# Edge arrays in rows of 2 KB, and routing and experts in one block: a graph layer on one core

## The reference

```python
xn = layernorm(x)
h = xn @ weight_l
agg = segment_sum(edge_weight[:, None] * h[dst], src, 12500)      # scatter-add by source
x = x + (agg + bias_l + xn @ weight_r + bias_r) + mix(xn)         # mix: linear attention, gated
xn2 = layernorm(x) * gamma + beta
logits = xn2 @ Wr + br                                            # 8 experts
top_vals, top_idx = top_k(logits, 2); w = softmax(top_vals)
out = x + sum over the two chosen experts e of w_e * (gelu(xn2 @ W1[e] + b1[e]) @ W2[e] + b2[e])
```

## Time and profile before

| | us |
|---|---|
| median of three runs | 4451.65 (4448.86 to 4453.43) |
| the profiled execution, its own time | 4440.3 |
| its span in the trace | 4438.6 |
| first scatter-add to the end of the last | 157.54 to 3257.14 |
| first instruction of the expert part on TensorE | 3651.79 |
| GpSimd busy | 3111.7 (70%) |
| TensorE busy | 3389.3 (76%), mean granted clock 0.864 |

### The profile page before, as it was taken

One profiled execution on the slowest core, in us unless ns is written; L12 is line 12 of the kernel. 1 busy time (PEld: TensorE's weight loads), 2 busy tenths in 40 slices (PEclk: granted clock), 3 DMA queues, 4 the chain that ended last, 5 costly groups with the idle time before them and its releaser, 6 DMA issues. The chain is left out here.

```text
span 4438.6 us, 85552 instructions
## 1 busy us (share of the span) xinstructions
PE 3389.3 (76%) x16628; PEld 2802.7 (63%) x16629; DVE 2495.7 (56%) x11386; ACT 1685.6 (38%) x3095; POOL 3111.7 (70%) x2088
## 2 busy tenths in 40 slices
PE   1466666667677677878888888888758859999998
PEld 1355555555565555666666666666557758888887
DVE  3577777665555555666666666666548862222222
ACT  1233333344444443444444444444312224444443
POOL 0488888888888888888888888888855544444444
PEclk7788878788888888888888888888779979999999
DMA  9888888877777777777777777777789965565554
GB/s 380 241 146 155 152 148 147 157 117 118 116 109 115 116 113 114 102 108 108 105 104 107 108 103 105 108 107 102 91 217 296 294 187 143 139 145 141 141 140 114
DMA packets 588869, 638.95 MB, mean 144 GB/s; under 512 B 60524, under 2 KB 553156, under 8 KB 587138
## 3 DMA queue, kind: packets, MB, share of 16 engines
q0 software_dynamic: 279264, 269.84, 48.5%
q1 hardware_dynamic: 262234, 273.19, 20.9%
q10 hardware_dynamic: 47304, 95.18, 5.9%
HBM read 249.82 MB, written 390.09 MB: 144 GB/s over the span
## 5 line engine op out<-in xcount | busy, mean ns | idle before, releaser
L818 POOL DMA_INDIRECT agg<-msg,sidx x1664 | 2585.7, 1554 | 667.5 <-issue 408.7
L1122 PE MATMUL bank<-rows,Cmat 128*128 x3328 | 1025.7, 450 | 166.7 <-ACT msg L1315 140.6
L1315 ACT COPY msg<-bank 128x512 f32<-128x512 f32 x832 | 487.1, 585 | 1486.0 <-DMA agg<-msg,sidx 1209.8
L1122 PEld LDWEIGHTS bank<-rows,Cmat 128*128 128x128 f32 x3328 | 699.1, 224 | 346.7 <-issue 253.8
L873 DVE SCALAR_TENSOR_TENSOR sidx<-seen_sum,trash,srcf 128x4 int32<-128x4 f32 x416 | 92.7, 223 | 1022.8 <-DMA agg<-msg,sidx 1017.6
L2069 POOL DMA_INDIRECT out_dram<-x_y,x_node x210 | 325.7, 1551 | 473.1 <-issue 228.2
L856 DVE TENSOR_SCALAR Emat<-bank,srcf,wtf 128x128 f32<-128x128 f32 x1664 | 564.5, 398 | 0.0
L1106 PEld LDWEIGHTS bank<-Emat,pick 128*128 128x128 f32 x3328 | 518.3, 226 | 41.6 <-issue 17.7
L1106 PE MATMUL bank<-Emat,pick 128*128 128x128 f32 x3328 | 528.7, 311 | 1.6 <-DVE seen L860 1.6
L1097 PE MATMUL bank<-packed,both 128*128 (+1 forms) x416 | 187.3, 451 | 437.9 <-DVE seen L860 427.9
L860 DVE SCALAR_TENSOR_TENSOR seen<-bank,srcf,prior 128x128 f32<-128x128 f32 x1664 | 479.1, 341 | 0.0
(11 more groups left out here) (245 smaller groups left out, 4130.6 us busy)
## 6 DMA issues: line engine op xcount, KB each, us to landing
x_w<-in_L_ffn_W_dram SPq DMA_DIRECT2D x105, 512.0 KB, 4.1
agg<-expert_rows ACTq DMA_DIRECT2D x12, 4224.0 KB, 63.3
r_agg<-agg SPq DMA_DIRECT2D x196, 256.0 KB
x_zin<-table SPq DMA_DIRECT2D x105, 259.0 KB, 4.1
window_raw<-in_x_dram SPq DMA_DIRECT2D x208, 128.0 KB, 2.5
agg<-msg,sidx POOLq DMA_INDIRECT x1664
xn_rows<-n_xn ACTq DMA_DIRECT2D x49, 256.0 KB
xn_turned<-n_xnT ACTq DMA_DIRECT2D x49, 256.0 KB
```

The lines of the kernel that those rows point to most:

```text
L818: pool.indirect_dma_start(scratch["agg"][r][:, :], bass.IndirectOffsetOnAxis(ap=sidx[:, j:j + 1], axis=0), msg[:, j % (2 * BATCH), :], Non ...
L1122: mm = nc.tensor.matmul(M[p][:, (q % 2) * D:(q % 2 + 1) * D], Cmat[:, b % 2, q, :], rows[:, bass.ds(slot, 1), :], start=True, stop=True)
L1315: nc.scalar.copy(msg[:, at:at + 2, :].rearrange("p q c -> p (q c)"), M[p][:, :]).then_inc(s_msg, 1)
```

## The change

It has four pieces.

The edge arrays are loaded in rows of 512 values (2 KB, `LONG`) instead of 128: `raw` and `flt` become [128, 4, 512], the last tile with a piece of 31 rows and one of 20 values (`load_end`). The array `wide` is no longer loaded: four masks on VectorE make it from `raw["src"]`. A tile holds four chunks to a row, so TensorE turns four parts of each tile (`turn_tile`), and the copies out of PSUM put the columns back in order (`chunks_of`, `turned_of`). Scan, plan and the stores of the plan follow the new shape (four stores instead of two).

The semaphores of the sends are doubled, a set for even pairs and one for odd ones: a send waits for the same send two pairs back (`turns_before`).

The empty rows are written with rows of 2,072 bytes instead of 1,036 (`"(p a) d -> p a d"`), and no engine waits for them at the end of routing.

Routing and experts stand in one block. What the barrier gave is waited for by name: each engine that reads the plan waits for the plan's 21 steps (`PLANNED`), and SyncE waits for fills, spare rows, stores of x and all sends (`table_complete`) right ahead of its first load of table rows. The weights' loads stand ahead of that wait.

```diff
-ETILES = CHUNKS // P
-EFULL = E // P
+LONG = BATCH * P
+LTILES = -(-CHUNKS // BATCH // P)
+LWINDOWS = P * BATCH // WINDOW
+LGROUPS = P * BATCH // CHUNK_GROUP
...
+PLANNED = 21
...
-        route_phase(nc, scratch, out, psum, ident, ones, iota8, lower, run, nodes, ffn, iotaq, base, offset, expert)
-        expert_phase(nc, t, scratch, out, psum, ident, iota8, offset, expert, ffn)
+        s_plan = sem("p_step")
+        block = ctx.enter_context(nc.Block())
+        table_complete = route_phase(nc, ctx, block, scratch, out, psum, ident, ones, iota8, lower, run, nodes, ffn, iotaq, base, offset,
+                                     expert, s_plan)
+        expert_phase(nc, ctx, block, t, scratch, out, psum, ident, iota8, offset, expert, ffn, s_plan,
+                     table_complete)
...
-        raw = {k: sb(f"raw_{k}", [P, ETILES, P], dt) for k, dt in (("src", I32), ("dst", I32), ("wt", F32))}
-        flt = {k: sb(f"flt_{k}", [P, ETILES, P]) for k in ("src", "dst", "loc")}
+        raw = {k: sb(f"raw_{k}", [P, LTILES, LONG], dt) for k, dt in (("src", I32), ("dst", I32), ("wt", F32))}
+        flt = {k: sb(f"flt_{k}", [P, LTILES, LONG]) for k in ("src", "dst", "loc")}
...
         def load_edges(engine, to, a, done):
             engine.dma_start(to[:, 0:full_tiles, :],
-                             a[0:full_tiles * P * P].rearrange("(t c p) -> c t p", c=P, p=P)).then_inc(done, 16)
-            engine.dma_start(to[0:rest_rows, full_tiles, :],
-                             a[full_tiles * P * P:EFULL * P].rearrange("(c p) -> c p", p=P)).then_inc(done, 16)
-            engine.dma_start(to[rest_rows:rest_rows + 1, full_tiles, 0:rest],
-                             a[EFULL * P:E].rearrange("(a p) -> a p", a=1)).then_inc(done, 16)
+                             a[0:full_tiles * P * LONG].rearrange("(t c e) -> c t e", c=P, e=LONG)).then_inc(done, 16)
+            load_end(engine, to[:, full_tiles, :], a, done)
+
+        def load_end(engine, to, a, done):
+            engine.dma_start(to[0:rest_rows, :],
+                             a[full_tiles * P * LONG:BFULL * LONG].rearrange("(c e) -> c e", e=LONG)).then_inc(done, 16)
+            engine.dma_start(to[rest_rows:rest_rows + 1, 0:rest],
+                             a[BFULL * LONG:E].rearrange("(a e) -> a e", a=1)).then_inc(done, 16)
+
+        def chunks_of(to, i):
+            n = P if i < full_tiles else LREST
+            return to[:, i * LONG:i * LONG + n * BATCH].rearrange("p (c r) -> p r c", r=BATCH), n
+
+        def turned_of(bank, n):
+            return bank[:, :].rearrange("p (r c) -> p r c", r=BATCH)[:, :, 0:n]
 
         @block.sync
         def _(sp):
...
-            act.wait_ge(s_clear, 5)
+            act.wait_ge(s_clear, 4)
...
-            tiles, long_row = BFULL // SPAN, BATCH * P
-            for half in (0, SPAN):
-                act.dma_start(wide[half:half + SPAN, 0:tiles, :],
-                              t["src"][0:tiles * SPAN * long_row].rearrange("(t c e) -> c t e", c=SPAN, e=long_row)
-                              ).then_inc(s_wide, 16)
-                act.dma_start(wide[half:half + BFULL % SPAN, tiles, :],
-                              t["src"][tiles * SPAN * long_row:BFULL * long_row].rearrange("(c e) -> c e", e=long_row)
-                              ).then_inc(s_wide, 16)
-                at = half + BFULL % SPAN
-                act.dma_start(wide[at:at + 1, tiles, 0:E - BFULL * long_row],
-                              t["src"][BFULL * long_row:E].rearrange("(a e) -> a e", a=1)).then_inc(s_wide, 16)
-            act.wait_ge(s_clear, 6)
+            act.wait_ge(s_clear, 5)
             for acc, n in clears[:READY]:
                 act.dma_start(clear_rows(acc, n), zeros).then_inc(s_zeroed, 16)
 
             act.wait_ge(s_src, 48)
             nc.scalar.copy(flt["src"][:], raw["src"][:]).then_inc(s_fsrc, 1)
...
-                for four in FOURS:
+                for i in range(LTILES):
                     act.wait_ge(s_turn, n + 1)
-                    nc.scalar.copy(to[:, four[0] * P:(four[-1] + 1) * P], psum[n % 4][:, 0:len(four) * P]).then_inc(s_taken, 1)
+                    chunks, held = chunks_of(to, i)
+                    nc.scalar.copy(chunks, turned_of(psum[n % 4], held)).then_inc(s_taken, 1)
                     n += 1
-            act.wait_ge(s_masked, 2)
+            act.wait_ge(s_masked, 4)
...
-            dve.wait_ge(s_wide, 96)
-            nc.vector.tensor_scalar(wide[0:SPAN], wide[0:SPAN], (P - 1) * P, None, ALU.bitwise_and).then_inc(s_masked, 1)
-            nc.vector.tensor_scalar(wide[SPAN:P], wide[SPAN:P], P - 1, None, ALU.bitwise_and).then_inc(s_masked, 1)
+            dve.wait_ge(s_src, 48)
+            upper, lower_half = raw["src"][0:SPAN], raw["src"][SPAN:P]
+            for to, bits in ((wide[0:SPAN], (P - 1) * P), (wide[SPAN:P], P - 1)):
+                nc.vector.tensor_scalar(to[:, 0:BTILES:2, :], upper, bits, None, ALU.bitwise_and).then_inc(s_masked, 1)
+                nc.vector.tensor_scalar(to[:, 1:BTILES:2, :], lower_half[:, 0:LTILES - 1, :], bits, None,
+                                        ALU.bitwise_and).then_inc(s_masked, 1)
...
+            def turn_tile(bank, a, i):
+                for r in range(BATCH):
+                    mm = nc.tensor.transpose(bank[:, r * P:(r + 1) * P], a[:, i, r * P:(r + 1) * P], ident[:])
+                return mm
...
-        s_sent = [[sem(f"r_sent{c}{m}") for m in range(2)] for c in range(2)]
+    s_sent = [[[sem(f"r_sent{s}{c}{m}") for m in range(2)] for c in range(2)] for s in range(2)]
...
+    def table_complete(engine):
+
+        for half in range(2):
+            engine.wait_ge(s_filled[half], 16 * NE // 2)
+        engine.wait_ge(s_spare, 16)
+        for s in range(2):
+            engine.wait_ge(s_x1st[s], 16 * ((PAIRS + 1 - s) // 2) + 16 * ((PAIRS - 1) % 2 == s))
+            for c in range(2):
+                for m in range(2):
+                    engine.wait_ge(s_sent[s][c][m], 16 * ((PAIRS + 1 - s) // 2))
+        engine.nop(nofuse=True)
+
...
+    def turns_before(i, u):
+
+        return i // 2 if isinstance(i, int) else (i - u) // DEPTH * (DEPTH // 2) + u // 2
...
-                engine.dma_start(scratch["table"][bass.ds(at, CAP), :].rearrange("(a p) d -> p a d", p=P),
+            engine.dma_start(scratch["table"][bass.ds(at, CAP), :].rearrange("(p a) d -> p a d", p=P),
                                  fill[:]).then_inc(s_filled[half], 16)
-            engine.wait_ge(s_filled[half], 16 * NE // 2)
...
-                        if not below(i, 1):
-                            pool.wait_ge(s_sent[c][m], 16 * i)
+                    if not below(i, 2):
+                        pool.wait_ge(s_sent[u % 2][c][m], 16 * turns_before(i, u))
                         pool.nop(nofuse=True)
                         pool.indirect_dma_start(scratch["table"][:, :],
                                                 bass.IndirectOffsetOnAxis(ap=pos[:, u % 2, c, m:m + 1], axis=0),
-                                                z[:, u, c, :], None).then_inc(s_sent[c][m], 16)
+                                            z[:, u, c, :], None).then_inc(s_sent[u % 2][c][m], 16)
 
...
+            if first(k) and s == 0:
+                sp.wait_ge(s_plan, PLANNED)
+                sp.nop(nofuse=True)
...
+            if first(k) and s == 0:
+                table_complete(sp)
...
+            if first(k) and s == 0:
+                pe.wait_ge(s_plan, PLANNED)
```

More of the change, by code:

```diff
@@ L332, in _ @@
             dve.wait_ge(s_pool, 3)
[L333 to L335 removed]
+            for i in range(LTILES):
+                for r in range(BATCH):
+                    chunk = flt["loc"][:, i, r * P:(r + 1) * P]
+                    last = nc.vector.scalar_tensor_tensor(out=chunk, in0=edges["iota"][:], scalar=tgen[:, i:i + 1],
+                                                          in1=chunk, op0=ALU.mult, op1=ALU.add)
             step(last)
```

1176 lines of the change are left out of this document (582 added, 594 removed).

## The result

| | before | changed |
|---|---|---|
| median of 18 runs | 4454.74 us (4448.86 to 4462.12) | 4462.4 us (4456.34 to 4467.86) |
| profiled execution, span | 4440.3, 4438.6 us | 4461.48, 4459.8 us |

The ratio of the changed kernel to the one before is 1.0017, 95% interval 1.0010 to 1.0024: 4.5 to 10.7 us slower, 7.6 in the middle. 4453 was predicted, with 4428 to 4466 as range; the time lies in it, on the slow side, and 1.4 us above the forecast's own range of 4446 to 4461.

What follows compares the result with a forecast made beforehand. GpSimd's 1,664 scatter-adds were taken as a block of fixed length, delayed by whatever delays its first adds. Setup +16, seam -10 and routing -5 gave +1 us, hence 4453 us, range 4428 to 4466.

Steps and rivals of the forecast that it cites:

- The fill and the early clears: Setup: without the wide loads the clears wait only for the zero fill, starting about 11.6 us instead of 24.54.
- The weights behind the clears: Setup: SyncE's weight loads get stuck beside ScalarE's early clears and land at 95.5 us instead of before 46.6.
- The exchange of one for one: DMA queues in setup: one entry of SyncE's q1 passes for each entry of ScalarE's q10, 1.25 us per clear row.
- the lone engine: Setup loads: all four 31-row end pieces fall on one DMA engine, whose clears begin only at 23.4 us.
- The gap: Setup: the last five clears wait behind ScalarE's copies until 104.5 us, queues idle ten to twenty us; cleared about 158.
- The edge block: Scatter-adds after setup: window load at 116, first add 170, third 177.4 instead of 161.40; setup costs +16 us.
- The seam: Between routing and experts: without the barrier TensorE starts at 3642.2 instead of 3651.8 us; -10 taken.
- Routing: Routing sends waiting two pairs back shorten VectorE's 10.5 us of waits; half taken, -5 us, bounds -10.5 and +3.
- The sum: Whole kernel: +16 - 10 - 5 = +1 us, 4441 by the profiled execution's clock, 4453 as median.
- 1 (the loads slip through): Setup: small loads pass in time, early clears are real, third add about 152.5; total -24, 4428 us; chance 0.20.
- 2 (the pieces on different engines): Setup: no engine carries 198 rows, everything behind comes 9 to 11 us sooner; total -9, 4443 us; chance 0.13.
- 3 (GpSimd's closing moves to the end): Program end: GpSimd's closing work moves there, price +8, tail over 10 us; 4462 us; chance 0.15.

Runs made afterwards that it cites:

- e6: The changed kernel with each clear's rows of 33.8 KB cut into three of 11.3 KB, same bytes; ratio to the kernel before 0.9965.
- e4: The changed kernel with ScalarE waiting for all fourteen weight loads before issuing the first seven clears; ratio to the kernel before 0.9971.
- e7: The changed kernel with each end piece of 31 rows loaded as 16 and 15 rows; ratio to the kernel before 0.9969.
- e1: The kernel before, unchanged, profiled a second time; median 4440.4 us, ratio 1.0000.
- e9: The kernel before, unchanged, profiled a third time on another chip; ratio 1.0000.
- e3: The changed kernel with one set of send semaphores, a send waiting for the same send one pair back; ratio to the kernel before 1.0011.
- e2: The changed kernel with the whole setup of the kernel before, so only routing and seam changed; ratio to the kernel before 0.9975.
- e10: The changed kernel with clears waiting for the weights and end pieces split 16 and 15, clears in full rows; ratio to the kernel before 0.9950.
- e12: The kernel of e10 with only the last two clears cut into rows of 11.3 KB; ratio to the kernel before 0.9953.
- e11: The kernel of e10 with the barrier between routing and experts put back; ratio to the kernel before 0.9964.

## Why the prediction was right, step by step

- **The fill and the early clears.** Predicted near 12 us, found at 13.35. Right.
- **The weights behind the clears.** 95.5 predicted, `bsum` at 96.64. The exchange of one for one is shown by e6 (other entry size) and e4 (no clears there), the lone engine by its six rows from 87 to 95 us and by e7. One count on the way was wrong: of the entries left in q1, 126 were stated, 92 by e6. In the changed kernel 27 entries of q1 passed from 95.10 to 95.43 us, when its clears had ended; with the 56 that passed beside the clears these are 83. It did not matter, since anything over the 56 entries of seven clears waits for their end.
- **The gap.** The first of the five clears was predicted at 104.5 and came at 109.66. The path from `bsum` was taken as before's 8.0 us plus 1; it was 13.0. ScalarE's copies, strided now, took 3.12 us per array instead of 1.73, and VectorE's of `locf` 1.95 for two instead of 1.27. The prediction had them at "about 1 us more, off the path unless I say so": they were on it, and the one us that it added there was too little. (e1 and e9 have 9.2 and 9.0 us for the same path before, so of the 4 us missed one is before's first profile.)
- **The edge block.** First window load at 119.17 (116 predicted), x in at 163.31 (160.5), first add 174.70 (170), third 180.66 (177.4). The window load's 3.2 us (1.1 of them from `bsum`, 2.1 from the path behind it) run through all of them. By this pair of profiles setup costs 19.3 instead of 16, by the third add. The means of three profiles each (161.40, 162.53, 162.72 and 180.66, 179.32, 178.52) give 17.3, the ratios 17.3 and 18.6, and e3 against e2 on one chip 15.7. The term was right within the 3 us or so that single profiles leave open.
- **The seam.** -10 predicted. From the last send to TensorE's start the three profiles of before have 17.7 us in the mean, e2, e3, e4, e10 and e12 7.4: -10.3. Routing and seam together went from 389.7 to 379.7, -10.0. The changed kernel's own profile, which is one with a slow pair, gained only 7.6. The mechanism was right in what it removed, the silence behind GpSimd's closing, but by e11 the barrier alone is worth only 5 of the ten.
- **Routing.** -5 predicted, nothing found (e3 against e4). This is the step that failed: waits for sends on VectorE were taken as time on the path. The trace had 10.5 us of them, and half of it seemed a cautious value; when the waits went, VectorE stood idle as long as before (32.7 us in 200 with either kind of send), and the pair stayed at 7.14 to 7.19.
- **The sum.** +1 predicted; 17.3 - 10 = +7.3 by the profiles, +7.6 (4.5 to 10.7) by time. Of the difference 5 are routing and 1 to 2 the path with the copies. The other 3 us between 4453 and 4462.4 are the base: before's median is 4454.74 over 18 runs, 4451.65 over the three that were known. The forecast's own range, to 4461, was missed by 1.4; it is the wide range, drawn to hold the rivals too, that holds the time. The prediction took 0.2% as what can be told from no change; the measured 0.17% is under that, but its interval (0.10 to 0.24%) leaves out no change.
- **The rivals.** 1 (the loads slip through) is out, `bsum` did not come at 40. 2 (the pieces on different engines) is out for the changed kernel and is what e7 makes of it: `bsum` at 85.97, where "85" was written. 3 (GpSimd's closing moves to the end) is out: the tail stayed 6.0 us, and the DRAIN at the program's end takes 8.5 us, where it took 8.8 before. The measured 4462.4 is just the 4462 written for rival 3. That is chance, and by its time alone the run would have spoken for the wrong mechanism.

## What to carry to other kernels

A large transfer issued early is not free, even on another queue: count the entries of what shares its DMA engines, not the bytes. Let the small loads that computation waits for land first, and start the bulk behind a wait on them; here that wait turned 0.17% slower into 0.29% faster than before, and 0.50% faster together with the cut end pieces. An end piece whose row count leaves it on one engine, as 31 rows did here, is worth cutting so that it spreads (16 and 15). A wait in a trace is worth its time only if nothing else stands ready to fill it. And before two profiles are compared, profile the first kernel on the second one's chip.

## What the hardware showed beyond this

Seven issues of a clear took ScalarE 7.6 us with 56 entries to an engine, 42.1 us with 168 (e6), so a queue seems to hold fewer than 168 entries, with the issuing engine standing until there is room and its computing behind it. For the same bytes larger entries thus spare the issuer and smaller ones the neighbour queue; e12 found no gain between them. The rate hardly suffered from the smaller rows: 8.48 MB in 20 us in e6 are 424 GB/s, against 433 in the changed kernel.
